# Routing and reciprocal roots once per two batches, W2 scaled on GpSimd, and the first expert tiles between the mixer's last steps

## The reference

```python
x = L0_attn_x                                    # (16, 512, 128)
sa, ca, ga, sb, cb, gb = split(silu(c) @ wmod)   # per batch, 128 each; |ga|, |gb| at least 0.25
h = layernorm(x) * (1 + ca) + sa
x = x + ga * mixer(h)    # xi = silu(h @ Win + bin); a scan over the 512 positions with decay 0.9;
                         # y = state @ Cp + Dp * xi; y @ Wout + bout
h = layernorm(x) * (1 + cb) + sb
# experts: 8 experts, the best 2 for each token
p = softmax(h @ Wr + br); probs, idx = top_k(p, 2); probs = probs / probs.sum()
y_e = layernorm(relu(layernorm(relu(h @ W1_e + b1_e)) @ W2_e + b2_e))     # 128 -> 512 -> 128
x = x + gb * sum over the two chosen e of prob_e * y_e
```

## Time and profile before

| | us |
|---|---|
| three runs | 647.34, 657.39, 656.96 |
| their median | 656.96 |
| the profiled execution | 647.95 |
| its span | 645.8 |
| mean granted clock of TensorE, as a share of 2.4 GHz | 0.912 |

### The profile page before, as it was taken

One profiled execution on the slowest core, in us unless ns is written; L12 is line 12 of the kernel. 1 busy time (PEld: TensorE's weight loads), 2 busy tenths in 40 slices (PEclk: granted clock), 3 DMA queues, 4 the chain that ended last, 5 costly groups with the idle time before them and its releaser, 6 DMA issues. The chain is left out here.

```text
span 645.8 us, 15964 instructions
## 1 busy us (share of the span) xinstructions
PE 542.2 (84%) x3102; PEld 411.9 (64%) x3103; DVE 486.6 (75%) x2313; ACT 416.5 (64%) x1126; POOL 341.6 (53%) x442
## 2 busy tenths in 40 slices
PE   2889878886878526978999999999999999997097
PEld 1445444444445414966898888898888898896042
DVE  5989667777577626756898888898888888889187
ACT  0457546555555213756788788888787887887386
POOL 3552656666465654255655655655555656566300
PEclk9999887888888655988999999999999999999589
DMA  6944111111111213121111111111111211110498
GB/s 182 306 151 105 47 41 39 46 42 42 34 47 42 73 39 115 51 55 47 54 58 52 55 53 53 57 53 53 55 51 53 57 47 56 49 51 34 153 369 267
DMA packets 60169, 52.23 MB, mean 81 GB/s; under 512 B 8902, under 2 KB 53177, under 8 KB 60006
## 3 DMA queue, kind: packets, MB, share of 16 engines
q1 hardware_dynamic: 51718, 34.92, 19.5%
q0 software_dynamic: 8416, 16.93, 7.3%
HBM read 29.67 MB, written 22.58 MB: 81 GB/s over the span
## 5 line engine op out<-in xcount | busy, mean ns | idle before, releaser
L493 POOL DMA_INDIRECT expert_rows<-rows,slot x128 | 124.1, 969 | 94.0 <-issue 49.7
L521 POOL DMA_INDIRECT expert_results<-y,target x135 | 134.0, 993 | 49.5 <-issue 48.6
L1190 PE MATMUL bank<-W,h2T 128*128 x1080 | 144.0, 277 | 1.0 <-ACT h2T L626 0.8
L1190 PEld LDWEIGHTS bank<-W,h2T 128*128 128x128 f32 x1080 | 132.4, 193 | 1.7 <-issue 1.7
L618 ACT ACTIVATE h1T<-bank 128x512 f32<-128x512 f32 x135 | 80.4, 596 | 55.4 <-PE bank L1177 49.9
L1006 DVE BATCH_NORM_STATS2 stf<-h1T 128x6 f32<-128x512 f32 x135 | 91.0, 674 | 0.0
L984 DVE SCALAR_TENSOR_TENSOR wmod<-bank,rse,c 128x128 f32<-128x128 f32 x135 | 47.4, 351 | 56.0 <-issue 29.2
L1181 PE MATMUL bank<-ident,h1T 128*128 128x128 f32 x540 | 82.3, 275 | 1.7 <-ACT h1T L618 1.7
L1181 PEld LDWEIGHTS bank<-ident,h1T 128*128 128x128 f32 x540 | 68.4, 143 | 21.4 <-ACT h1T L618 2.5
L626 ACT ACTIVATE h2T<-bank 128x512 f32<-128x512 f32 x135 | 79.1, 586 | 0.3 <-PE bank L1181 0.3
L1174 PE MATMUL bank<-b_parts,onesr 128*128 x135 | 66.1, 489 | 5.5 <-DVE h3lo L998 3.6
(11 more groups left out here) (203 smaller groups left out, 1106.7 us busy)
## 6 DMA issues: line engine op xcount, KB each, us to landing
hrow<-expert_rows SPq DMA_DIRECT2D x135, 65.0 KB
X<-in_L_attn_x SPq DMA_DIRECT2D x8, 512.0 KB, 7.4
W<-expert_results SPq DMA_DIRECT2D x8, 512.0 KB, 6.4
out_x<-X SPq DMA_DIRECT2D x16, 256.0 KB, 5.3
expert_results<-y,target POOLq DMA_INDIRECT x135
expert_rows<-rows,slot POOLq DMA_INDIRECT x128
xi<-expert_results SPq DMA_DIRECT2D x4, 512.0 KB, 7.2
b_parts<-expert_results SPq DMA_DIRECT2D x4, 512.0 KB, 7.5
```

The source lines that it names most:

```text
L493: nc.gpsimd.indirect_dma_start(out=rows_d, out_offset=bass.IndirectOffsetOnAxis(ap=slot[q][:, n // TOPK, n % TOPK:n % TOPK + 1], axis=0), ...
L521: nc.gpsimd.indirect_dma_start(out=results_d, out_offset=bass.IndirectOffsetOnAxis(ap=target[n % TURN][:], axis=0), in_=y[k][:], in_offset ...
L1190: ins = mm(acc, rT[q][:, ch * P:(ch + 1) * P], W2[:, bass.ds(e2 * CF + ch, 1), :], start=(ch == 0), stop=(ch == CF - 1))
```

## The change

1. Step s of stage 1 now takes the first statistics of batch s + 4, and reciprocal roots are made in even steps only, sixteen columns at once, for the batches s - 2, s - 1, s + 2 and s + 3 (s from -2 on); in the same place VectorE puts the four statistics of batch s + 4 between the root instructions. The normalisation of the second norm comes a step later (batch s - 3).
2. Logits, maxima and indices stay per batch (batch s - 4), but everything after them, from `hot` to `slot`, and the rank matmuls, run in odd steps for a pair of batches. RING is 8, there are four `slot` buffers.
3. GpSimd scales W2 in 16 instructions of 128 x 512 before its first scatter; VectorE's part goes.
4. ROUND1_BATCHES is 8, which makes 56 tiles of round 1. The scatters are written out; 100 come before the first result, and the last 28 stand one by one behind the results of tiles 0 to 27.
5. Stage 1 has steps -4 to 19. Its last four (16 to 19) are placed before the expert steps -1, 1, 3 and 5. For that the tiles use other PSUM banks (`bank[3]`, `bank[0]` and `bank[4]` once each instead of in pairs, with new waits for the reader), `rT` lies in `n1`, `vs` has 16 buffers in `mixT` and `n2`, there are 16 `target` buffers and TURN is 16, so tiles up to 31 are written out. Round 2's count is made in expert step 6 instead of before the tiles.
6. SP loads three turns of eight tiles before it turns to the gate rows and the padding.

```diff
--- before.py
+++ after.py
...
-    ROUND1_BATCHES = 10
+    ROUND1_BATCHES = 8
...
+        RING = 8
+        ring = sb("ring", [P, RING * J, ROW])
+        rows = [ring[:, k * J:(k + 1) * J, :] for k in range(RING)]
+        b1f, b1hi, b1lo = [ring[0:E, k * J:(k + 1) * J, :].rearrange("p j d -> p (j d)")[:, 0:F] for k in (5, 6, 7)]
+        b1hi = b1hi.bitcast(F32R)
+        b1lo = b1lo.bitcast(F32R)
+        JJ = 2 * J
+        PAIRS = B // 2
+        SLOT_RING = 4
...
-        VS = 8
...
+        VS = 16
...
-        FIRST1, LAST1 = -2, B + 2
-        TURN = 8
+        FIRST1, LAST1 = -4, B + 3
+        TAIL = {-1: B, 1: B + 1, 3: B + 2, 5: B + 3}
+        TURN = 16
...
                 for s in range(begin, end):
+                    if s in TAIL:
+                        tail_step(TAIL[s], TAIL[s] % 2)
                     step(s, s % TURN, lambda k: loaded[s + k - start])
...
+            with sp.Fori(1, 3) as turn:
+                for n in range(SLOTS):
+                    load_next(turn * SLOTS + n, n)
             sp.wait_ge(gb_stored, 16)
-            sp.wait_ge(w2_ready, B)
+            sp.wait_ge(w2_ready, E)
             sp.dma_start(gb_rows[:], gates_d.rearrange("o (b d) -> o b d", b=B).broadcast_to([P, B, D])).then_inc(gb_loaded, 16)
             sp.wait_ge(counts_ready, 1)
...
+            pool.wait_ge(sums_loaded, 32)
+            for e in range(E):
+                part = slice(e * CF, (e + 1) * CF)
+                nc.gpsimd.tensor_tensor(W2[:, part, :], W2[:, part, :],
+                                        g1T[:, part].rearrange("p (c o) -> p c o", o=1).broadcast_to([P, CF, D]),
+                                        ALU.mult).then_inc(w2_scaled, 1)
+            for e in range(E):
+                part = slice(e * CF, (e + 1) * CF)
+                pool.wait_ge(w2_scaled, e + 1)
+                nc.gpsimd.tensor_tensor(W2[:, part, :], W2[:, part, :],
+                                        means[:, e:e + 1, :].broadcast_to([P, CF, D]), ALU.subtract).then_inc(w2_ready, 1)
+            def scatter(m):
+                b, n = m // (J * TOPK), m % (J * TOPK)
+                if n == 0:
+                    pool.wait_ge(rows_ready, b + 1)
+                    pool.wait_ge(ids_ready, b // 2 + 1)
+                    pool.wait_ge(slot_ready, b // 2 + 1)
+                    pool.nop(nofuse=True)
+                j, k = n // TOPK, n % TOPK
                 nc.gpsimd.indirect_dma_start(
-                    out=rows_d, out_offset=bass.IndirectOffsetOnAxis(ap=slot[q][:, n // TOPK, n % TOPK:n % TOPK + 1], axis=0),
-                    in_=rows[q][:, n // TOPK, :], in_offset=None).then_inc(rows_stored[q], 16)
-            def store_batch(b, q):
-                rows_of(b)
-                for n in range(J * TOPK):
-                    store_rows(q, n)
-            with pool.Fori(0, B // RING - 1) as four:
-                for k in range(RING):
-                    store_batch(four * RING + k, k)
-            for b in range(B - RING, B - 1):
-                store_batch(b, b % RING)
-            rows_of(B - 1)
+                    out=rows_d, out_offset=bass.IndirectOffsetOnAxis(
+                        ap=slot[b // 2 % SLOT_RING][:, b % 2 * J + j, k:k + 1], axis=0),
+                    in_=rows[b % RING][:, j, :], in_offset=None).then_inc(rows_stored[b % RING], 16)
+            SCATTERS = B * J * TOPK
+            LATE = ROUND1 // 2
+            for m in range(SCATTERS - LATE):
+                scatter(m)
...
                 for n in range(count):
-                    add_shift(turn * TURN + n, n, first and n < RESULTS, expert[n])
-                    if first:
-                        store_rows((B - 1) % RING, n)
-                    if n > 0 or not first:
-                        store_results(turn * TURN + n - 1, (n - 1) % TURN)
-            assert J * TOPK == TURN
-            turn_of_results(0, TURN, True)
-            pool.wait_ge(table_ready, 2)
-            with pool.Fori(1, EXPERT_TILES // TURN) as turn:
-                turn_of_results(turn, TURN, False)
-            turn_of_results(EXPERT_TILES // TURN, EXPERT_TILES % TURN, False)
+                    i = turn * TURN + n
+                    add_shift(i, n, isinstance(i, int) and i < RESULTS, expert[n])
+                    if not isinstance(i, int) or i > 0:
+                        store_results(i - 1, (n - 1) % TURN)
+                    if isinstance(i, int) and i < LATE:
+                        scatter(SCATTERS - LATE + i)
+            PLAIN = (ROUND1 + TURN - 1) // TURN
+            for turn in range(PLAIN):
+                if turn == ROUND1 // TURN:
+                    pool.wait_ge(table_ready, 2)
+                turn_of_results(turn, TURN)
...
+                pair = (s - 5) // 2
+                route = q == 1 and on(pair, PAIRS)
+                norm = q == 0 and (on(a, B) or on(s + 2, B))
+                now, cols = s // 2 % 2, slice(0 if on(a, B) else JJ, 2 * JJ if on(s + 2, B) else JJ)
+                mv_a, mv_b = (s + 1) // 2 % 2, ((s + 1) // 2 if q == 1 else s // 2 + 1) % 2
...
+                if route:
+                    dve.wait_ge(besti_ready, u + 1)
                     vec.tensor_tensor(
-                        hot[p][:], iota_e[:].rearrange("p (a b e) -> p a b e", a=1, b=1).broadcast_to([P, J, TOPK, E]),
-                        besti[p][:, :, 0:TOPK].rearrange("p j (k o) -> p j k o", o=1).broadcast_to([P, J, TOPK, E]),
+                        hot[v][:], iota_e[:].rearrange("p (a b e) -> p a b e", a=1, b=1).broadcast_to([P, JJ, TOPK, E]),
+                        besti[v][:, :, 0:TOPK].rearrange("p j (k o) -> p j k o", o=1).broadcast_to([P, JJ, TOPK, E]),
                         ALU.is_equal).then_inc(hot_ready, 1)
...
+                if route:
+                    dve.wait_ge(rank_done, pair + 1)
+                    if c == ROUND1_BATCHES:
+                        vec.tensor_copy(cnt_i[:], bank[7][:, COUNTS])
...
+                if norm:
+                    if on(s + 2, B):
+                        dve.wait_ge(mv1_ready, s + 4)
+                    if on(a, B):
+                        dve.wait_ge(mv2_ready, s)
+                    vec.tensor_scalar(ve[now][:, cols], mv[now][:, cols, 1], EPS, None, ALU.add).then_inc(ve_ready, 1)
...
+                    square(0)
+                    if s > 0:
+                        stats1(2)
+                    times_v(0)
+                    if s > 0:
+                        stats1(3)
+                    refine(0)
+                    square(1)
+                    if s > 0:
+                        aggr1(0)
+                    times_v(1)
...
-                if on(s - 3, B):
-                    if isinstance(s, int) and s == 3:
-                        dve.wait_ge(sums_loaded, 32)
-                    for m in range(2):
-                        n = (s - 3) * 2 + m
-                        ins = vec.scalar_tensor_tensor(W2[:, bass.ds(n, 1), :], W2[:, bass.ds(n, 1), :], g1T[:, bass.ds(n, 1)],
-                                                       means[:, bass.ds(e - 2 + q, 1), :], ALU.mult, ALU.subtract)
-                    ins.then_inc(w2_ready, 1)
...
-            pe.wait_ge(carry_ready, B)
-            pe.wait_ge(x1_ready, B)
-            mm(bank[5][:, 0:E], ones[:], carry[:], start=True, stop=True).then_inc(count_done, 1)
-            pe.wait_ge(place_ready, B)
-            pe.wait_ge(rows_ready, B)
-            pe.wait_ge(w2_ready, B)
+            pe.wait_ge(w2_ready, E)
...
+                if isinstance(s, int) and s == 6:
+                    pe.wait_ge(carry_ready, PAIRS)
+                    pe.wait_ge(x1_ready, B)
+                    mm(bank[5][:, 0:E], ones[:], carry[:], start=True, stop=True).then_inc(count_done, 1)
...
```

More of the change, by code:

```diff
@@ L107, in adaln_ssm_moe_kernel @@
         be1_g1m = sb("be1_g1m", [P, E * CF, 2])
+        RESULTS = 4
+        y = [sb(f"y_{q}", [P, D]) for q in range(RESULTS)]
+        c_sb, c_act, gb_sign, gb_abs = [t[0:B, :] for t in y]
         means = gb_rows
@@ L137, in adaln_ssm_moe_kernel @@
         mixT = [sb(f"mixT_{q}", [P, L]) for q in range(2)]
[L139 to L145, removed]
+        st1 = [sb(f"st1_{q}", [P, J, 6]) for q in range(2)]
@@ L161, in adaln_ssm_moe_kernel @@
+        placed = [sb(f"placed_{m}", [P, JJ, TOPK, E]) for m in range(2)]
+        slot = [sb(f"slot_{m}", [P, JJ, TOPK], I32) for m in range(SLOT_RING)]
         cnt = sb("cnt", [P, E])
@@ L298, in run, with run_tiles @@
         def run(step, first):
-            for s in range(first, LAST1 + 1):
-                step(s, s % 2, s // 2, s % RING)
-        def run_tiles(engine, step, name=None, experts=None, oldest=0):
+            for s in range(first, min(TAIL.values())):
+                step(s, s % 2)
+        def run_tiles(engine, step, tail_step, name=None, experts=None, oldest=0):
             def load(start, count):
@@ L938, in mixer_step @@
-                if isinstance(s, int) and s == 1:
```

(13 more changed lines are left out.)

446 lines of the change are left out of this document (231 added, 215 removed).

## The result

The changed kernel takes 704.91 us (median of four runs, 701.21 to 709.54) where the kernel before, beside it, takes 653.98 us (four runs, 647.34 to 657.39): the ratio is 1.082, 95% interval 1.069 to 1.095. The profiled execution lasted 709.54 us with a span of 707.1 us, 61.3 us over the span before.

What follows compares the result with a forecast made beforehand. TensorE bounds the tile loop; scatter streams without a pause hold back the mixer. Terms -3 + 18 + 1 + 30 = +46 us on span 645.8 give 692, plus 2.1 is 694 us; range 605 to 715, likeliest case 665 to 715.

Steps and rivals of the forecast that it cites:

- Mechanism and sign: Scatter streams without a pause hold back the other engines until drained; bursts of 16 and late scatters make the kernel slower, +46 us.
- by bursts: Rival: each scatter burst costs the same 3.8 us whatever its length, so fewer bursts make it faster, 601.5 us; chance 0.25.
- Up to step 5: Mixer before the slots of step 5: less early work and bursts against statistics and W2 on GpSimd, -3 us.
- +7 us over my sum: Step 4's root chain: by the port lock rule, GpSimd's W2 instructions cost VectorE nearer the upper bound, some +7 us more.
- Five pairs: Mixer steps 5 to 15: bursts of 16 make a pair of steps 30 us against 26.4, +18 us.
- undisturbed pair: Two mixer steps without scatter delays after the change: 17.6 us instead of 18.7, limited by TensorE.
- 0.7 us for matmuls: In each pair of mixer steps: 0.7 us added for matmuls at half clock after the standstill.
- The overlap of the last four steps: Slots of step 15 to tile 6: last four mixer steps among the first tiles, 50.7 us against 49.7, +1.
- 28 late scatters: Round 1 tiles: 28 carry a scatter beside their result where 8 did; 20 more at 1.48 us, +30 us.
- short losses in the mixer, late scatters at full price: Rival: mixer gains 34.6 us, late scatters cost 30, so 643 us, no change to tell; chance 0.17.
- The tile loop: Tile loop after the late scatters: bound by TensorE, its work left as it is, so 0 us.
- the port decides: Rival: two-input VectorE instructions of steps 3 to 5 all wait for GpSimd, 9 us more, 703 us; chance 0.04.

Runs made afterwards that it cites:

- experiment 1: Kernel before, with GpSimd holding an even batch's scatters until the odd one's slots are there, so bursts of 16: 685.61 us beside 648.96, ratio 1.061.
- experiment 3: Kernel before plus GpSimd work in the tile loop: indirect DMA every tile 814.13 us, every second tile 731.7, plain DMA 646.19, addition 742.49; unchanged 648 to 649.
- Experiment 5: Changed kernel (703.65 us) with 8 late scatters in place of 28: 706.17 us; separately, with W2 scaling back on VectorE: 692.4 us.
- experiments 5 and 6: Scatters moved: changed kernel with 8 late scatters in place of 28, ratio 1.095; kernel before with the last batch's eight issued ahead of the tiles' results, 0.996.
- Experiment 4: Changed kernel with the tile loop over 8 tiles in place of 16 (TURN and VS 8): 698.41 us beside 648.96, ratio 1.081.

## Why the prediction was right, and where it was not

**Mechanism and sign** held. Bursts of 16 were the dearest item, as read from one burst of the kernel before, and experiment 1 gives them alone 36.6 us. The rival *by bursts* is refuted by it. The Trainium skill's rule beside this rival (SBUF — State Buffer, section "SBUF: two separate sides": a DMA and an engine's instruction don't slow each other) agrees with the plain DMA of experiment 3, where nothing was lost, and not with the indirect ones, with 84 and 165 us lost.

**Up to step 5**, -3 forecast, -2.0 measured. The W2 instructions took 1.06 and 1.29 us in order of time for an estimated 1.26, and VectorE's first four root instructions of step 4 1.1 us each for an estimated 1.2: four, not seven. Three of them read two SBUF tensors, and so waited as the Trainium skill's rule of the lock between VectorE and GpSimd (the same page and section) has it. Experiment 5 gives their price as 5.4 us for the estimated 7, so the +7 us over my sum that I had drawn from that rule didn't come.

**Five pairs**, +18 forecast, +22.2 measured (30.8 us each for 30). A run of 16 costs 13.2 us where I had read 11.7 from the one burst seen; taken off 30.8 that leaves the 17.6 us of the undisturbed pair that I had estimated, but no run shows the changed kernel's pair undisturbed. The 0.7 us for matmuls assumed half clock throughout; in the second pair the mean granted clock is 0.74 in the last 7 us before the engines resume and 0.64 in the 7 us after, between the two levels.

**The overlap of the last four steps**, +1 forecast, -2.1 measured (47.6 us from the slots of step 15 to tile 6, for 50.7).

**28 late scatters**, +30 forecast, +25.0 measured between tiles 6 and 37: with a tile in 3.6 us there (111.71 us for 31). For each of the 20 more that is 1.25 us where I had read 1.48. That the price belongs to late scatters was wrong: experiments 5 and 6 moved them and saved little or nothing. The rival *short losses in the mixer, late scatters at full price* rested on the same mistake.

**The tile loop**, 0 forecast, +18.7 measured between tile 37 and the last. This step failed. I wrote that the change leaves the loop's work and what follows it as they are; it leaves the work, but doubles the code of a turn (`TURN = 16`), and I put no price on that. The kernel before showed a little of it, 0.5 us a turn, which I did not read. Experiment 4 gives some six tenths of the term to the length of the body.

The median came out at 704.9 for a forecast of 694, and this one missing term is more than the difference. Luck has a part in how near the rest is: up to tile 37 it is +43.2 for +46, because the pairs' +4 and the late scatters' -5 nearly cancel. It is luck too that the rival *the port decides*, with 703 us, lies nearer than my own figure: the slots of step 5 came at 81.95 us for the 81 forecast, not 9 us later.

## What to carry to other kernels

Count how many indirect DMAs GpSimd issues without a pause before you batch or delay them: here two runs of 8 cost 7.7 us and one of 16 cost 13.2, and moving scatters to another place saved little or nothing as long as they stood in a run. Don't expect a gain from saving VectorE's instructions in a step that GpSimd's scatters already fill (20.2 us of a 26.4 us pair): none was seen here, and with the W2 scaling back on VectorE four pairs took 26.2 us each, for 30.2 with it on GpSimd. No run made the saving with the bursts left as they were. When a diff changes how far a loop is unrolled, price the turn: read the gap at a turn in the trace of before, and look at the instruction queues' packets in the trace after.

## What the runs showed of the hardware that I had not expected

- GpSimd's indirect DMAs hold up TensorE, VectorE and ScalarE where a plain DMA from the same queue doesn't: with 1.5 indirect DMAs a tile in place of one TensorE's busy time in 150 us fell from 149.94 to 132.32 us, with one plain DMA added to 149.05.
- The onset is sooner than I had read: in the tile loop VectorE came to rest 3.2 us after the first of six indirect DMAs, and idled for 5.6 us.
- A tile loop whose body was twice as long lost 4 to 6 us at each turn, with instruction packets on one queue rising from 24 to 57 in the whole kernel, 20 of them in four turns of the loop; with the short body they were 26, and none in the loop from 470 to 590 us.
- A GpSimd addition of 128x512 in each tile made VectorE the bound of a loop that TensorE had bounded: 340 ns an instruction for 228.
